# A transformer block on one core: who squares the gelu's blocks

## The reference

```python
x = x + _layernorm(attn(_layernorm(x)))       # 16 heads of 32, rotary by head, causal softmax
x = x + _layernorm(ffn(_layernorm(x)))
def bitlinear(x, w):                          # in ffn, forward value
    xn = (x - mean(x)) / sqrt(var(x) + 1e-6)  # over features
    gamma = max(|xn|)
    x_hat = clip(xn * 128 / gamma, -128 + eps, 128 - eps) * gamma / 128
    return x_hat @ (sign(round(w / (mean(|w|) + eps))) * mean(|w|)).T
def ffn(x):
    h = gelu(bitlinear(x, w_fc))              # 512 -> 2048
    return bitlinear(h, w_proj)               # 2048 -> 512
```

## Time and profile before

| what | value |
|---|---|
| median of 3 runs | 1350.2 us (1348.36 to 1352.62) |
| the profiled execution | 1350.0 us, span 1348.2 us |
| mean granted clock of TensorE | 0.955 of full speed |
| busy: TensorE, VectorE, ScalarE, GpSimd | 89%, 76%, 58%, 44% of the span |

### The profile page before, as it was taken

The page is one execution under the profiler, slowest core; times in us unless marked ns, Lnnn a source line. Parts: engine busy times, 40 slices in busy tenths (PEclk is TensorE's granted clock), DMA queues, the critical chain, the costliest instruction groups (busy, mean ns, idle before and its releaser), DMA issues.

```text
span 1348.2 us, 25057 instructions
## 1 busy us (share of the span) xinstructions
PE 1203.6 (89%) x9388; PEld 652.2 (48%) x9388; DVE 1020.3 (76%) x2931; ACT 780.8 (58%) x1446; POOL 594.2 (44%) x636
## 2 busy tenths in 40 slices
PE   4755889999999999999999999999999999988796
PEld 2322555455545554455545554455545554554343
DVE  7588797868877797878887797868887787777532
ACT  3334864666556664666456755666466755575480
POOL 5231441692049502791149412781159412871252
PEclk9865888999999999999999999999999999999799
DMA  5351121002310113002310113002300221001000
GB/s 203 124 158 57 42 69 55 1 2 56 95 40 3 36 52 102 1 4 66 83 40 2 43 46 102 1 12 68 86 27 3 56 60 44 2 3 55 8 1 31
DMA packets 49685, 65.37 MB, mean 48 GB/s; under 512 B 8439, under 2 KB 33047, under 8 KB 49052
## 3 DMA queue, kind: packets, MB, share of 16 engines
q1 hardware_dynamic: 49564, 63.78, 16.1%
HBM read 29.90 MB, written 8.39 MB: 28 GB/s over the span
## 4 chain that ended last, share of the span: by engine, by line
PE 54%; DVE 30%; ACT 8%; issue 3%; POOL 3%; SPq 1%; DMA 1%; POOLq 0%; DVEq 0%; ACTq 0%
PE gen L476 22%; PE down L519 16%; DVE score L1075 8%; PE pv L573 5%; PE score L545 4%; DVE hT L942 4%; PE score L551 2%; DVE acc_add L1052 1%; POOL rstd L1407 1%; DVE bn L1104 1%; DVE qkn L1167 1%; DVE mx L1075 1%; PE gen L536 1%; DVE probs L942 1%; ACT qkn L736 1%
## 5 line engine op out<-in xcount | busy, mean ns | idle before, releaser
L1407 POOL TENSOR_TENSOR rstd<-veps,mhalf 128x1 f32<-128x1 f32 (+1 forms) x104 | 68.3, 657 | 486.6 <-DVE veps L1152 373.9
L792 ACT ACTIVATE probs<-score 128x512 f16<-128x512 f32 (+1 forms) x384 | 201.9, 526 | 127.4 <-PE score L545 127.4
L942 DVE TENSOR_TENSOR probs<-score,probs 128x512 f16<-128x512 f32 (+1 forms) x384 | 213.2, 595 | 69.2 <-ACT score L794 69.2
L476 PE MATMUL gen<-x2T,t1T 128*128 128x512 f16 x1024 | 242.1, 381 | 5.9 <-DVE hT L942 3.4
L519 PE MATMUL down<-t2T,hT 128*128 128x512 f16 x1024 | 232.9, 380 | 3.5 <-DVE xn L1137 3.5
L794 ACT ACTIVATE score<-score 128x512 f32<-128x512 f32 (+1 forms) x384 | 204.8, 533 | 0.0
L476 PE MATMUL gen<-xT,wa 128*128 128x512 f16 x768 | 180.4, 386 | 11.2 <-DVE wa L962 7.5
L942 DVE TENSOR_TENSOR hT<-gen,hT 128x512 f16<-128x512 f32 x160 | 108.4, 684 | 73.3 <-ACT gen L755 31.6
L1075 DVE CUSTOM_DVE_ANT_0 score<-score,mask_rows 128x512 f32<-128x512 f32 (+1 forms) x344 | 157.6, 519 | 0.0
L519 PEld LDWEIGHTS down<-t2T,hT 128*128 128x128 f16 x1024 | 96.5, 98 | 110.3 <-DVE xn L1137 4.7
L476 PEld LDWEIGHTS gen<-x2T,t1T 128*128 128x128 f16 x1024 | 96.2, 98 | 111.0 <-DVE hT L942 5.3
(11 more groups left out here) (131 smaller groups left out, 1842.2 us busy)
## 6 DMA issues: line engine op xcount, KB each, us to landing
qk<-qkn SPq DMA_DIRECT2D x384, 64.0 KB, 2.0
xo<-x SPq DMA_DIRECT2D x8, 1024.0 KB, 5.7
hT<-x SPq DMA_DIRECT2D x8, 1024.0 KB, 6.4
out<-xn SPq DMA_DIRECT2D x32, 256.0 KB, 2.2
hT<-w_fc SPq DMA_DIRECT2D x4, 1024.0 KB, 6.8
hT<-w_down SPq DMA_DIRECT2D x4, 1024.0 KB, 5.6
hT<-w_attn SPq DMA_DIRECT2D x4, 512.0 KB, 10.1
hT<-w_attn SPq DMA_DIRECT2D x1, 1024.0 KB, 8.7
```

The source lines that it names most:

```text
L476: mm = nc.tensor.matmul(bank[:, :], a, b, start=(start and n == 0), stop=(stop and n == len(pairs) - 1))
L792: nc.scalar.activation(probs[:, h % 2, HI, 512 * i:512 * i + n], score[i][:, 0:n], ACT.Exp, scale=1.0 / S_UP)
L942: return V.tensor_tensor(out, whole, hi, ALU.subtract)
```

## The change

In the stages with `here`, ScalarE now also squares each block, as it did in the last stage: it waits for its own second gelu, squares the bank (ACT.Square, f32) into a buffer, and this third instruction raises `h_full`. Block 0 goes straight into `acc`; the others into a ring of four buffers of 512 f32 that lie in the memory of `probs`. GpSimd adds one buffer per block to `acc`. Before writing buffer u ScalarE waits, from u = 5 on, for the addition of block u-4. The exponents of heads 0 and 1, which write into the same memory, wait for the additions up to block 13 and for all of them. The last stage computes as before. The whole diff:

```diff
--- before.py
+++ after.py
@@ -238,6 +238,7 @@
         b_row, b_r1, b_r2 = (temp[0:1, 4096 + 1024 * i:5120 + 1024 * i] for i in range(3))
         vb_in, pb_in = temp[:, 7168:7680], temp[:, 7680:8192]
         rope_sb = probs[:, 0, :, :].rearrange("p a n -> p (a n)").bitcast(f32)[:, 0:2 * E]
+        squared = probs[:, :, :, :].rearrange("p r a n -> p r (a n)").bitcast(f32)
         m_stage = acc[:, 0:PARTS]
         t16 = acc_add[:, :].bitcast(f16).rearrange("p (r e) -> p r e", r=2)
         below = acc[:, :].bitcast(f16).rearrange("p (r e) -> p r e", r=2)
@@ -247,7 +248,7 @@
         gen = [ctx.enter_context(nc.psum_tensor(f"gen{i}", [PARTS, 512], f32)) for i in range(3)]
         pv = ctx.enter_context(nc.psum_tensor("pv", [PARTS, 512], f32))
         down = ctx.enter_context(nc.psum_tensor("down", [PARTS, 512], f32))
-        SQ_STEPS = 3 * FC
+        SQ_STEPS = FC - 1
         H_SUM, H_SQ = 264, 268
 
 
@@ -293,6 +294,14 @@
         sq_step, out_ready = sem("sq_step"), sem("out_ready")
 
         signs = down[:, :].bitcast(f16)
+
+        def square_of(u, here):
+
+            if u == 0:
+                return acc[:, :]
+            if not here:
+                return xn[:, u % 2, :]
+            return squared[:, u % 4 // 2, 512 * (u % 2):512 * (u % 2) + 512]
 
         def block_at(s, tb):
 
@@ -502,7 +511,7 @@
                 def square_sums():
 
 
-                    pe.wait_ge(sq_step, SQ_STEPS * j if here else SQ_STEPS * (j - 1) + FC - 1)
+                    pe.wait_ge(sq_step, SQ_STEPS * j)
                     for tb in range(TB):
                         mm = nc.tensor.matmul(pv[:, H_SQ + tb:H_SQ + tb + 1], acc[:, PARTS * tb:PARTS * (tb + 1)],
                                               ones32[:, 0:1], start=True, stop=True)
@@ -753,14 +762,12 @@
                     bank = filled("up", u)
                     nc.scalar.activation(hT[:, HI, u, :], bank[:, :], ACT.Gelu, scale=gam[:, 0:1])
                     whole = nc.scalar.activation(bank[:, :], bank[:, :], ACT.Gelu, scale=gam[:, 0:1])
-                    if not here:
-
-                        whole.then_inc(gelu_done, 1)
-                        if u >= 3:
-                            act.wait_ge(sq_step, SQ_STEPS * (j - 1) + u - 2)
-                        act.wait_ge(gelu_done, u + 1)
-                        whole = nc.scalar.activation(xn[:, u % 2, :] if u else acc[:, :], bank[:, :], ACT.Square)
-                    whole.then_inc(h_full, 1)
+                    whole.then_inc(gelu_done, 1)
+                    ring = 4 if here else 2
+                    if u > ring:
+                        act.wait_ge(sq_step, SQ_STEPS * (j - 1) + u - ring)
+                    act.wait_ge(gelu_done, FC * (j - 1) + u + 1)
+                    nc.scalar.activation(square_of(u, here), bank[:, :], ACT.Square).then_inc(h_full, 1)
 
                 def normalise(tb):
                     nc.scalar.activation(xn[:, tb % 2, :], xo[:, tb, :], ACT.Identity, bias=shift[:, LX, tb:tb + 1],
@@ -787,6 +794,8 @@
 
                 def exponents(h):
 
+                    if prev and h < 2:
+                        act.wait_ge(sq_step, SQ_STEPS * j - 2 * (1 - h))
                     for i, n in enumerate(SCORE_W):
                         act.wait_ge(s_full, s0 + S["scores", h] + i + 1)
                         nc.scalar.activation(probs[:, h % 2, HI, 512 * i:512 * i + n], score[i][:, 0:n], ACT.Exp,
@@ -1416,24 +1425,11 @@
 
                 def squares(u):
 
-                    if not here:
-                        if u:
-                            pool.wait_ge(h_full, FC * (j - 1) + u + 1)
-                            if u >= 2:
-                                pool.wait_ge(sq_step, SQ_STEPS * (j - 1) + u - 1)
-                            P.tensor_tensor(acc[:, :], acc[:, :], xn[:, u % 2, :], ALU.add).then_inc(sq_step, 1)
-                        return
-                    pool.wait_ge(g_drained, g0 + G["up", u] + 1)
-                    n = SQ_STEPS * (j - 1) + 3 * u
                     if u:
-                        pool.wait_ge(sq_step, n)
-                    whole = acc_add if u else acc
-                    P.tensor_tensor(whole[:, :], hT[:, HI, u, :], hT[:, LO, u, :], ALU.add).then_inc(sq_step, 1)
-                    pool.wait_ge(sq_step, n + 1)
-                    P.tensor_tensor(whole[:, :], whole[:, :], whole[:, :], ALU.mult).then_inc(sq_step, 1 if u else 2)
-                    if u:
-                        pool.wait_ge(sq_step, n + 2)
-                        P.tensor_tensor(acc[:, :], acc[:, :], acc_add[:, :], ALU.add).then_inc(sq_step, 1)
+                        pool.wait_ge(h_full, FC * (j - 1) + u + 1)
+                        if u >= 2:
+                            pool.wait_ge(sq_step, SQ_STEPS * (j - 1) + u - 1)
+                        P.tensor_tensor(acc[:, :], acc[:, :], square_of(u, here), ALU.add).then_inc(sq_step, 1)
 
                 def under(n):
```

## The result

| | before | after |
|---|---|---|
| median beside each other on one chip | 1350.7 us | 1360.1 us (1358.6 to 1361.0) |
| ratio | | 1.0072, 95% interval 1.0059 to 1.0085 |
| profiled execution, span | 1350.0, 1348.2 us | 1358.6, 1356.8 us |

I had predicted 1355.0 us, in a range of 1349 to 1362: slower, as it came, by 4.8 us, where it is 9.3.

The account below looks back on a forecast made before the run. Stages bound by VectorE and TensorE in turn: locked stages 4 x (0.87 - 0.57) = 1.2, unlocked 2 x (0.87 + 0.53) = 2.8, stage 7 0.8; +4.8 on 1350.0 gives 1354.8, median 0.2 higher: 1355.0 us, range 1349 to 1362.

Parts of the forecast that it names:

- GpSimd's saved work: In seven stages, GpSimd's over 2.4 us less a block for 15 blocks would be worth 0 by itself.
- the four locked stages: Stages 1, 3, 4 and 5, where GpSimd delays VectorE's cast before `scores(0)`: 6.25 us becomes 5.68, gaining 0.57 each.
- none would wait before `scores(0)`: Sign at the end of stages 1 to 6: cast at 0.4 to 0.7 us, no wait before `scores(0)`.
- The ring: ScalarE's wait for the addition four blocks ago: GpSimd, at 1.27 us a block, would never be so late.
- It cancels: Rival: VectorE's own waits in the blocks shrink the 0.87 shift to 0.4; +1.7 us, 1352; chance 0.30.
- It is faster: Rival: low halves don't wait for the square, VectorE's queue being late; lock's relief gives 4.8 us, 1345.4; chance 0.10.
- ScalarE's order becomes the bound: Rival: extra ScalarE work at blocks 8, 10, 12, 15 makes TensorE wait 0.64 each; 15.4 us more, 1370; chance 0.10.
- Exponents 0 wait for addition 13 ... there is over 1 us to spare: Before the heads: additions end at about 585, first exponents not before 586.2, so the new wait costs nothing.
- The start of a stage, +0.87: First low half 0.64 later, second 0.85, block 7's 0.85 to 0.9: +0.87 us a stage, bounds 0 and 1.3.
- The credit of 0.3 for `veps`: In the moments, `veps` (0.82 us under GpSimd's load) meets a shorter addition and gives back 0.3 us.
- The end, 5.68 from the old start of block 14's low half: Stage end up to `scores(0)`: 0.64 shift, 0.72 to the transposition, 4.32 more; 5.68 us.
- Stage 7: Without moments and normalisations: 0.64 at the start plus 0.15 at the end, +0.8 us.

Follow-up runs that it names:

- e3: Changed kernel with the square reading the f16 high half from SBUF, so the second gelu again raises `h_full`; 1345.9 us, ratio 0.9992 to the kernel before.
- e5: Kernel before, plus a tiny Gelu activation behind each iteration's last ScalarE copy, to load the table early; 1343.3 us, ratio 0.9946.
- e1: Changed kernel with a tiny Exp activation ahead of the exponents of head 0; 1357.9 us, ratio 1.0076 to the kernel before.
- e2: Changed kernel with the two normalisations taken apart, one behind block 6, one behind block 7; 1357.5 us, ratio 1.0072 to the kernel before.
- e4: Kernel before with the first two of GpSimd's three instructions per block left out (variance wrong); 1345.5 us, ratio 0.9988.
- e9: The changed kernel itself, run once more on another chip; 1360.3 us, ratio 1.0101 to the kernel before.
- e8: Changed kernel, square still from the bank, with the normalisations apart and tiny Exp and Gelu preloads; 1344.3 us, ratio 0.9960 to the kernel before.
- e10: Changed kernel with the ring's wait moved from ahead of the square to ahead of the first gelu; 1360.3 us, ratio 1.0097 to the kernel before.
- e7: Changed kernel with the square of the high half, the normalisations apart and tiny Exp and Gelu preloads; 1335.2 us, ratio 0.9889 to the kernel before.

## Why the prediction was right in direction and half in size

**Right.** The stage is bound by what VectorE and TensorE pass each other, and a low half that comes later moves it (table; e3, e5 from both sides). GpSimd's saved work is worth nothing by itself, only through the lock, that is through VectorE's conversions waiting for GpSimd's instruction to end. That lock is real and was worth what I said: in three of the four locked stages 6.25 became 5.15 us, in stage 3 5.49. By the Trainium skill, "SBUF — State Buffer", "Who interferes with whom", the blocked engine waits until the other's instruction is over. The trace agrees: after, the cast ends at 433.46, GpSimd's addition at 433.38:

```profile
432.11 1.27 POOL L1432 TENSOR_TENSOR acc<-acc,probs 128x512 f32<-128x512 f32 x1 [1.07 <-ACT probs L770]
```

The first six stages became alike up to block 14's low half; that none would wait before `scores(0)` failed in stage 3. The ring never held ScalarE up, and the waits for the additions before the exponents were met in time, as said.

**The rivals.** "It cancels" needed low halves with slack; +1.12 us at block 9 and +1.81 at block 14 say that the shift is not taken up. "It is faster" stood on the first wait not growing: it grew from 1.87 to 2.50. "ScalarE's order becomes the bound" had no part as put, at blocks 8, 10, 12 and 15; but its idea, work of ScalarE in front of a block that is wanted, is what happened at block 7, and I had sized it too small.

**Where the 4.9 us between forecast and result in six periods (4.0 and 8.9) sit**, 0.8 us a stage:
- *"Exponents 0 wait for addition 13 ... there is over 1 us to spare"*: the wait itself was free, but it pushed the wait for the scores onto the Exp's table load. 0.31 us a stage (e1). This was no wrong size but a missing step: the prediction asked only whether the new wait would be met in time.
- *The start of a stage, +0.87*: measured +1.12. I let the bank of block 6 come 0.65 us later; ScalarE began its gelu 0.89 us later (409.10 - 391.97 = 17.13 against 16.24 before), and each square from block 5 on has the second wait in front of it, 0.07 us. The pair began at 18.95 instead of 17.39, +1.56, where I had +1.29. e2 shows this point to be worth 0.6 us a stage. The credit of 0.3 for `veps` was about right in size and wrong in place. It reaches TensorE at `up(8)`, which is 0.49 us later than before, where I had about 0.55 just ahead of that point; `up(6)`, in front of it, is 0.89 later, the full delay of the start, and the pair of normalisations hangs on that bank. `up(8)` in stage 2 after and before (starts 391.97 and 392.55):

```profile
411.56 1.89 PE L485 MATMUL gen<-x2T,t1T 128*128 128x512 f16 x8
```
```profile
411.65 1.89 PE L476 MATMUL gen<-x2T,t1T 128*128 128x512 f16 x8
```

- *The end, 5.68 from the old start of block 14's low half*: that low half came 0.05 us later still, and from it to `scores(0)` it was 5.15, not 5.04: the transposition starts 0.83 us behind it (432.90 - 432.07), as it always did, and not 0.72.

These add to 0.31 + 0.25 + 0.05 + 0.11 = 0.72 us of the 0.8, and the late rows of stage 3, 0.33 us once, make 0.06 more. The forecast's total of +4.8 us thus has its direction and about half its size from the right places; its range was wide enough for the rest. Some of the closeness is luck: the 1.7 us that the profiled execution gained up to stage 1 have nothing to do with the change.

**Stage 7** was forecast at +0.8 and its period went from 133.3 to 134.6. Over the twelve profiles that period lies between 132.3 and 135.3 with no order in the changes (e4, with less work, 134.3; e5 135.3), so I draw nothing from it. The scatter lies behind the first `weigh`, though (87.8 to 90.7 us from there to the next stage), and in front of it the numbers repeat: `scores(0)` comes at 40.86 instead of 39.55, the first `weigh` at 46.16 instead of 44.54, +1.62 in after and e9 alike. The term was therefore half of what it should have been. It took 0.64 for the start alone, where the second low half, with no moments behind it, moved by 1.23.

## What to carry to other kernels

An instruction moved onto a half-idle engine is paid for at the points where that engine hands over, not in its busy share: put the new instruction behind the semaphore that others wait for. If it reads what the consumer reads too, give it another source, as e3 does at the price of the low halves. And before adding a wait in front of a function of another table, look at what carries the waits in the instruction order: an early dummy activation keeps the load off the path, and here the Gelu's alone was worth 7.8 us in six periods (e5, ratio 0.9946). e8 has these lessons without changing what is squared, and ends 0.4% under the kernel before.

## What the runs showed of the hardware that I had not expected

- Two waits ahead of a ScalarE instruction that needs another table: one sits on the load, which then runs in the open: 3.08 us of idle before it in after, 2.13 before the gelu's load in both kernels. "ScalarE: Activation LUTs" of the Trainium skill, "What ACT_TABLE_LOAD costs", has 1283 ns for the load, and the trace agrees (1.28); the section adds a drain of 1380 ns to each switch, and here the measurement differs. Behind the load nothing shows (it ends at 395.33, the first gelu starts at 395.34). Ahead of it neither: in e1 ScalarE's copy ends at 436.62, the load starts at 436.64 and the next activation at 437.93, 1.31 us for the whole switch.
- A wait that was long met still costs 0.07 us: with the ring's wait in front of it beside the one for the second gelu, the square starts at 0.75 instead of 0.68, and with that wait moved away (e10) at 0.68 again.
- A cast of 0.22 us took 0.48, 1.02 or 1.25 us, by where GpSimd's addition stood when it started: in each of these the cast ends 0.08 us behind the addition.
- In the heads of stage 7 TensorE's granted clock, 1.00 (2.4 GHz) through the blocks, falls to the lower level (1.2 GHz) for part of the time, sooner in some profiles than in others. Windows of the 20 us behind the first `weigh`, e7 and after; the clock is the third number from the end. TensorE was busy for 17.9 and 17.5 us of them, and for 39.6 and 38.7 of the 40 us at the stage's start, at 1.00. In the next 20 us the clock is 0.83 in both:

```profile
1173.20:1193.20 20.00, 17.86 (x198) 11.04 (x196) 14.29 (x37) 15.68 (x36) 0.00 (x0) 0.91 0.01 2
```
```profile
1195.00:1215.00 20.00, 17.46 (x201) 10.19 (x200) 14.99 (x39) 15.73 (x37) 0.00 (x0) 1.00 0.01 2
```

What sets the moment stays open. It does not order the periods of stage 7: e5 has 0.91 in that window too, and the longest period of all.
